# Edge stage of a graph kernel: the second product before the gathering of equal destinations, high casts on ScalarE, and the sort's numbering inside the stage

## What is computed

```python
e   = relu(edge_attr @ We1 + be1) @ We2 + be2            # 40000 x 256, hidden 512
msg = relu(layernorm(x)[src] + e)
out_h = segment_sum(msg, dst, num_segments=2500)
x = x + relu(((1 + eps) * layernorm(x) + out_h) @ Wn1 + bn1) @ Wn2 + bn2
```

## Time and profile before

| | us |
|---|---|
| median of 3 runs | 2723.11 (2719.55 to 2726.37) |
| the profiled execution | 2718.02 |
| its span | 2716.3 |

### The profile page before, as it was taken

One profiled execution on the slowest core, in us unless ns is written; L12 is line 12 of the kernel. 1 busy time (PEld: TensorE's weight loads), 2 busy tenths in 40 slices (PEclk: granted clock), 3 DMA queues, 4 the chain that ended last, 5 costly groups with the idle time before them and its releaser, 6 DMA issues. The chain is left out here.

```text
span 2716.3 us, 46328 instructions
## 1 busy us (share of the span) xinstructions
PE 2088.1 (77%) x13095; PEld 1804.4 (66%) x13096; DVE 1647.1 (61%) x4774; ACT 1007.2 (37%) x1931; POOL 1394.8 (51%) x1131
## 2 busy tenths in 40 slices
PE   2599999999999999955629999990466666662778
PEld 2588888888888888855628888880444444441776
DVE  5477786666666666648464444445655555557774
ACT  1254445545445554432205555550222222221321
POOL 1387887877777877760001111105377777771000
PEclk9799999999999999977759999995777767765888
DMA  6466656666666666642116777762233333342001
GB/s 165 134 131 131 133 120 130 134 132 135 135 128 125 133 130 133 129 86 70 39 41 229 244 243 242 239 220 81 76 92 93 90 89 91 90 84 28 22 10 38
DMA packets 185998, 325.71 MB, mean 120 GB/s; under 512 B 27528, under 2 KB 109037, under 8 KB 185192
## 3 DMA queue, kind: packets, MB, share of 16 engines
q0 software_dynamic: 82080, 141.73, 25.8%
q1 hardware_dynamic: 102962, 181.83, 21.8%
q10 hardware_dynamic: 900, 1.50, 0.2%
HBM read 260.65 MB, written 64.30 MB: 120 GB/s over the span
## 5 line engine op out<-in xcount | busy, mean ns | idle before, releaser
L632 POOL DMA_INDIRECT edge_sums<-edge_agg,edge_slot x316 | 551.3, 1745 | 172.5 <-issue 78.8
L1750 POOL DMA_INDIRECT att_got<-head_table,att_idx x352 | 401.8, 1141 | 125.1 <-issue 107.0
L623 POOL DMA_INDIRECT edge_nf<-node_table,edge_node_idx x316 | 327.3, 1036 | 152.0 <-issue 89.0
L751 ACT ACTIVATE edge_whole<-edge_h_ps,edge_b 128x512 f32<-128x512 f32 x316 | 215.8, 683 | 482.2 <-PE edge_h_ps L468 478.4
L466 PE MATMUL edge_e_ps<-edge_w_high,edge_hid_low 128*128 128x256 f32 x1264 | 357.3, 283 | 0.1
L467 PE MATMUL edge_e_ps<-edge_w_low,edge_hid_high 128*128 128x256 f32 x1264 | 356.9, 282 | 0.0
L468 PE MATMUL edge_e_ps<-edge_w_high,edge_hid_high 128*128 128x256 f32 x1264 | 356.2, 282 | 0.0
L1780 PE MATMUL att_s_ps<-att_w,att_hot 128*125 128x258 f32 x704 | 277.0, 562 | 3.2 <-issue 1.8
L466 PE MATMUL edge_h_ps<-edge_eat_high,edge_w_low 128*128 128x512 f32 x632 | 248.9, 394 | 23.6 <-DVE edge_eat_low L811 23.6
L1361 POOL DMA_INDIRECT moe_rows<-node_table,moe_idx x54 | 51.9, 961 | 396.8 <-DVE moe_idx L1473 396.4
L825 DVE TENSOR_TENSOR edge_pre<-edge_e_ps,edge_nf 128x1024 f32<-128x1024 f32 x79 | 96.8, 1225 | 256.2 <-DMA edge_nf<-node_table,edge_node_idx 208.9
(11 more groups left out here) (344 smaller groups left out, 4424.4 us busy)
## 6 DMA issues: line engine op xcount, KB each, us to landing
moe_w<-in_L_ffn_w_dram SPq DMA_DIRECT2D x162, 512.0 KB, 4.7
edge_ea<-in_edge_attr_dram SPq DMA_DIRECT2D x77, 448.0 KB, 5.1
edge_dst_row<-dst_rows SPq DMA_DIRECT2D x79, 256.0 KB, 4.5
routed<-moe_out SPq DMA_DIRECT2D x54, 128.0 KB, 6.3
att_got<-head_table,att_idx POOLq DMA_INDIRECT x352, 2.8
edge_nf<-node_table,edge_node_idx POOLq DMA_INDIRECT x316
edge_sums<-edge_agg,edge_slot POOLq DMA_INDIRECT x316, 4.8
edge_ea<-in_edge_attr_dram SPq DMA_DIRECT2D x77, 64.0 KB, 5.3
```

What stands on the lines that cost most here:

```text
L623: pool.indirect_dma_start(nf[u][:, j, :], None, m.node_table[:, :], bass.IndirectOffsetOnAxis(ap=node_idx[u][:, j:j + 1], axis=0)).then_in ...
L632: pool.indirect_dma_start(m.sums[k][:, :], bass.IndirectOffsetOnAxis(ap=slot[u][:, j:j + 1], axis=0), agg[u][:, j, :], None, compute_op=AL ...
L751: act.activation(whole[c][:], h_ps[:, c % 2, 0:N], ACT.Relu, bias=b1[:, c:c + 1]).then_inc(hid_whole, 1)
L1750: pool.indirect_dma_start(got[v][:, j, :], None, m.head_table[:, :], bass.IndirectOffsetOnAxis(ap=idx[v][:, j:j + 1], axis=0)).then_inc(la ...
```

## The change

- `edges_out(g)` stands ahead of `gather_same(g-1)` on TensorE, in all groups.
- ScalarE makes the high part of all four hidden pieces, each right after its relu, and the high part of the message after the fourth. VectorE's casts go.
- VectorE does `hidden_low` of pieces 0 and 1 ahead of `add_nodes(g-1)`, and `message_low(g-1)` after piece 3.
- The sort's numbering leaves `node_mlp`. After group 23 TensorE forms the totals in `h_ps` and waits until VectorE has read them (`offsets`); in groups 24 to 43 VectorE numbers one bucket each (`number_bucket`), and after that writes the slots out (`write_out`). TensorE's loop is cut in two there; VectorE's groups 22 to 43 are written out.
- The weights of `node_mlp` are loaded from ScalarE's queue.

```diff
@@ BucketSort
+    def offsets(self, dve, sums):
+        dve.wait_ge(self.summed, 1)
         chain.link(nc.vector.tensor_scalar(self.nblk_i[:], sums[0:LANES, 1, 0:buckets], (unit - 1) / 2, 1 / unit, ALU.add, ALU.mult))
+        chain.link(nc.vector.tensor_copy(off[:], sums[0:LANES, 0, 0:buckets]))
+        if self.by_bucket:
+            nc.vector.sem_inc(self.offsets_ready, 1)
...
+    def number_bucket(self, dve, b):
+        one = slot[:] if b == 0 else self.part_i[:].bitcast(F32)
+        units = self.m.count[0:1, 0:self.units]
+        last = self.last[0:1, b:b + 1]
+        chain.link(nc.vector.scalar_tensor_tensor(one, self.seen[:, b, :], self.off[:, b:b + 1], self.mask[:, b, :], ALU.add, ALU.mult))
+        if b == 0:
+            chain.link(nc.vector.tensor_scalar(tile_f[:], units, last, None, ALU.is_ge))
         else:
+            nc.vector.tensor_tensor(slot[:], slot[:], one, ALU.add)
+            chain.link(nc.vector.scalar_tensor_tensor(tile_f[:], units, last, tile_f[:], ALU.is_ge, ALU.add))
@@ edge_messages, TensorE
+    numbered = 2 + TILES + 2
...
+                edges_out(1)
                 pe.wait_ge(rows_made, 1)
                 gather_same(0, 0, first=True)
-                edges_out(1)
...
+                            edges_out(g + u)
+                            gather_same(g + (u - 1), 1 - u)
+                turns(2, numbered)
+                pe.wait_ge(hid_whole, numbered * KH)
+                by_src.order.totals(pe, h_ps)
+                pe.wait_ge(by_src.order.offsets_ready, 1)
+                turns(numbered, tail)
                 for g in range(tail, groups):
                     hidden(g)
                     if g + 1 < groups:
                         transposes((g + 1) % 2, ((g + 1) // 2 + 1) * 32)
+                    edges_out(g)
                     gather_same(g - 1, (g - 1) % 2)
-                    edges_out(g)
@@ ScalarE
                 for c in range(KH):
                     hidden_relu(g, c)
-                    if c == 1 and first != 1:
-                        message_high(g - 1)
-                    if c % 2 == 0:
-                        even_high(g, c)
+                    hidden_high(g, c)
+                if first != 1:
+                    message_high(g - 1)
@@ VectorE
             def hidden_low(g, c):
-                if c % 2 == 0:
-                    nc.vector.wait_ge(even_high_ready, g * (KH // 2) + (c // 2 + 1))
-                else:
-                    nc.vector.wait_ge(hid_whole, g * KH + (c + 1))
-                    nc.vector.tensor_copy(hidh[:, c, :], whole[c][:]).then_inc(odd_high_ready, 1)
-                    nc.vector.wait_ge(odd_high_ready, g * (KH // 2) + (c // 2 + 1))
+                nc.vector.wait_ge(hid_high_ready, g * KH + (c + 1))
...
+                    hidden_low(g, 0)
+                    hidden_low(g, 1)
                     add_nodes(1 - u, g - 1)
                     if ahead > 0:
                         stage_node_idx(1 - u, g + 1)
-                    hidden_low(g, 0)
-                    hidden_low(g, 1)
-                    message_low(g - 1)
                     hidden_low(g, 2)
                     hidden_low(g, 3)
+                    message_low(g - 1)
...
-                with dve.Fori(1 + TILES // 2, tail // 2) as turn:
+                for g in range(2 + TILES, numbered):
+                    one_group(g, g % 2)
+                by_src.order.offsets(dve, h_ps)
+                for g in range(numbered, numbered + TILES):
+                    one_group(g, g % 2)
+                    by_src.order.number_bucket(dve, g - numbered)
+                by_src.order.write_out(dve)
+                with dve.Fori((numbered + TILES) // 2, tail // 2) as turn:
@@ node_mlp
-                sp.dma_start(w1[:], io["Wn1"].rearrange("(k p) h -> p k h", p=P)).then_inc(w_in, 16)
...
-                by_src.order.number(dve)
...
+                act.dma_start(w1[:], io["Wn1"].rearrange("(k p) h -> p k h", p=P)).then_inc(w_in, 16)
...
-                by_src.order.totals(pe)
```

More of the change, by code:

```diff
@@ L275, in number @@
[L275 to L278 removed]
+        nc.tensor.matmul(sums[0:LANES, 0, 0:buckets], m.before[0:LANES, 0:LANES], self.mine[:], start=True, stop=True)
@@ L325, in _ @@
             def _(pe):
-                order.totals(pe)
+                order.totals(pe, order.sums)
             @block.vector
```

87 lines of the change are left out of this document (37 added, 50 removed).

## The result

The changed kernel takes **2745.8 us** (median of 4 runs, 2744.5 to 2753.1) against 2722.4 us (4 runs) before: 1.009 times the time, 95% interval 1.0068 to 1.0113. The forecast was 2685 us, with a range of 2645 to 2722. The sign was wrong.

The account below looks back on a forecast made before the run. The prediction took GpSimd, never resting in the edge stage at 14.07 us a group, as the bound. Steady part -30, start +5, numbering +3 and node stage -16 sum to -38 us from 2723.1: 2685 us, range 2645 to 2722.

Parts of the forecast that it names:

- steady part: 76 edge-stage groups at 13.7 us each in place of 14.1: -30 us (bounds -57 and +8).
- "These lie in its idle time": Numbering in 20 edge groups, 1.3 us each, hidden while VectorE waits for gathers; 26 us if the cover is gone.
- GpSimd's instructions without casts: Edge stage: without VectorE's casts GpSimd's adds and gathers take 0.6 us less a group, giving a floor of 13.1 us.
- x + B = 13.7: Edge group's pace: 6.8 us from `add_nodes` to the load, plus 6.9 from the load to the next `add_nodes`.
- its check: Two-group loop: 11.8 us first add to last gather, 5.4 gather, 10.2 `add_nodes` to first add; 27.4, again 13.7 a group.
- rival (c): Edge stage slower from late sums: two-group loop 29.5 us, 14.75 a group, +41 us in all, 2764 us; chance 0.14.
- gather + w: Gather's time plus an add's wait for a landing; from 6.4 us on the two-group loop reaches 14.2 a group.
- Start +5: GpSimd's first groups begin about 5 us later, the first gathering standing behind group 1's second product: +5 us (0 to 6).
- PE's wait for the offsets +3: TensorE waits once for `offsets_ready` in the edge stage, `hidden(24)` queued behind it: +3 us (0 to 6).
- Node stage -16: Node stage: third `combine` and TensorE's third turn 19.5 us earlier, less 3 us for slower clock: -16 us (-10 to -32).
- moving the weights "costs nothing": Node stage: moving three loads from SyncE's queue to ScalarE's costs nothing, since ScalarE has nothing else to do there.
- Rival (a): TensorE sets the edge pace, 13.35 us a group, if loads are early enough: -65 us in all, 2658 us; chance 0.20.

Follow-up runs that it names:

- e2: The changed kernel with the three edge edits undone, leaving the numbering in the edge stage and the node weights on ScalarE's queue: 2721.9 us, 1.001.
- e1: The kernel before with all edge edits (product order, casts on ScalarE, VectorE's and ScalarE's new orders), numbering left in the node stage: 2739.2 us, 1.0081.
- e13: The changed kernel with four slot buffers in place of two: 2739.7 us, 1.0056.
- e16: e14 with the sum of a bias to x in 20 pieces, one in each counting group, in place of one instruction: 2667.4 us, 0.9795.
- e4: The kernel before with only the high casts of all four tiles on ScalarE: 2735.1 us, 1.0056.
- e17: e14 with the odd high casts back on VectorE, ScalarE casting the even tiles only: 2681.8 us, 0.9866.
- e11: The changed kernel with edge rows loaded one group earlier and the node weights on SyncE's queue ahead of the sums: 2705.8 us, 0.9936.
- e14: The changed kernel with four slot buffers, edge rows loaded one group earlier and the node weights on SyncE's queue: 2672.1 us, 0.9805.
- e12: Old edge order, early edge rows, sorting in the edge stage, weights on SyncE's queue; `message_low` made a plain difference: 2693.1 us, 0.9891 (without that 0.9889).
- e5: The changed kernel with the sorting work ahead of `find_slots`' wait: eight of twelve runs 2724 to 2753 us (1.0046), four 2803 to 2838.
- e7: The kernel before with edge rows loaded one group earlier, ahead of the `dst_row` load: 2705.5 us, 0.9946.
- e3: The kernel before with only TensorE's order changed, second product ahead of gathering: 2922.8 us, 1.0759.
- e8: The kernel before with TensorE's and VectorE's orders changed, odd casts left on VectorE, message's high part after the second tile: 2954.6 us, 1.0859.

## Why the prediction was wrong, step by step

In short: the largest miss is the steady part, and in it the stretch B, from the load to the next `add_nodes`: forecast 6.9 us, measured 7.5. Over 76 groups that is 46 us. Two smaller ones are the numbering (11 us for the forecast's 3, for VectorE's idle time was taken as its cover) and the node weights (6.4 us gained of 16, for their move was put at nothing).

**"These lie in its idle time"** (numbering): failed for the order in which it was to be judged. It was true of the old order (e2: 1.001). The forecast took VectorE's idle share from before, 61% busy, but the change itself moves that idle time from ahead of `add_nodes` into `find_slots`, and the sorting work and the low parts stand behind it. The price was not 20 times 1.3 us but stood in two places, offsets 6.7 and writing out 4.5. In a third, the bias, the edge edits cost 5.0 (e1 has it without the numbering); the forecast didn't treat it, since the change doesn't touch it. Four slot buffers took the first two away (e13), pieces the third (e16). That a pause of TensorE in the edge stage is followed by matmuls at half the clock, 2.7 us at the offsets, was in no term; the forecast had the clock in the node stage alone.

**GpSimd's instructions without casts** (0.6 us a group, first add to last gather 11.8 us): failed. From first add to last gather it measured 12.6 us in the mean; of the 0.8 us more, 0.5 is in the adds, 0.1 in the gathers and 0.3 in the pauses between them. The row of 2.54 us with a cast in it showed that something beside an instruction lengthens it, not that the cast did: in the changed kernel an add of 2.68 us (1006.43) has no cast near. The Trainium skill's rule ("SBUF — State Buffer", two separate sides), by which a VectorE copy in a mode that takes both port pairs keeps GpSimd from writing descriptors, would have given up to 1.0 us a group, as the prediction has it. e4 and e17 show a loss of 0.35 us for GpSimd's adds in one order (4 x 0.087) and a gain of 0.17 in the other (4 x 0.042).

**x + B = 13.7**, and its check: x was right (6.8 us forecast and measured), B was 7.5, not 6.9. The forecast held B at 6.9 as long as the load is ahead of the gather. The loads were ahead, by 1.9 and 1.0 us (1.5 forecast), but the gather still took 5.6 us in the mean (5.4 forecast) and came later, since the stretch in front of it was longer. From `add_nodes` to the first add 10.4 (10.2). So the two-group loop is 12.6 + 5.6 + 10.4 = 28.6 us by the means of these parts, 14.3 a group, which is what the thirty groups from 44 on took; the forecast had 27.4. In e11, with the gather down to 3.5 us, the same parts are 12.2 + 3.5 + 11.3 = 27.0, and its groups there take 13.5. That is rival (c)'s loop, which was to take over from gather + w = 6.4 on; gather + w is 5.6 here, and what brings the loop to its length is the longer stretch from first add to last gather: the mechanism right, its deciding term another. Steady part: +16 us and the three places (16 more, the forecast's +3 in them), not -30; with the start (4.1) and all behind the last add (-7.6) that is the 28.5 us.

**Start +5**: 4.1. Right. **PE's wait for the offsets +3**: 4.2 us, but GpSimd's interval grew by 6.7; the slower clock behind the wait has 2.7 of it.

**Node stage -16, moving the weights "costs nothing"**: the sums' part of the step was right, the weights' was wrong. On ScalarE's queue they run beside the sums' loads, and the bias landed 26.6 us after its issue. With them on SyncE's queue the stage ends 15.0 us sooner after the last add than before (96.5 against 111.5): the -16 of the forecast. In the changed kernel 6.4.

**Rival (a)**, TensorE at 13.35 us "if the loads are far enough ahead": e14 and e16, where they are, run at 13.4, with 0.4 us of the wait for the last low part that was forecast at 0.45. The gather behind the edge rows took 5.4 us and without them 3.4: neither the full delay behind them nor none. The Trainium skill ("DMA: Bandwidth & Descriptors", queues, rings and completion order) has each DMA engine take turns between queues; the 5.4 us, between 3.4 and the 6.9 of a full wait, agree with sharing, and the share was got rid of by issuing the loads earlier.

What stays open: what lengthens GpSimd's instructions (e12 excludes one kind of neighbour; two SBUF inputs fit `message_low` and `add_nodes`, not `hidden_low`, and are not shown), and why e5's times fall into two sets.

## What to carry to other kernels

Reordering moves an engine's idle time, so ask, after the reorder, which wait it lies in and what is queued behind that wait; work is hidden only ahead of it. A change in an order that spans three engines is one unit: in parts it cost 203, 232 and 98 us here, whole 20, and with the sorting moved too 53 us less than before once the transfer that stood in the new loop and a two-deep buffer were out of the way. A pause of TensorE costs more than its length where the granted clock drops behind it. A load moved to another queue isn't free if it was first and now shares the DMA engines with large ones.

## What the runs showed of the hardware that was not expected

- A gather of node rows took 3.5 us in the mean (e7) with no edge rows (448 and 64 KB) issued beside it, and 5.4 with them (before); an add into a sum table took up to 8.8 us to land beside them (e13).
- Behind a pause of 4.2 us TensorE's granted clock was 0.50 from 434 to 440 us, and a hidden product took 8.3 us in place of 5.6. In the two slowest orders, in which TensorE waits most, the mean from 300 to 1100 us was 0.91 (e3) and 0.90 (e8).
- Three loads on a second queue, issued together with eight sum loads on SyncE's, landed 26.6 us after issue; ahead of the same loads on one queue 4.6 us.
- GpSimd's gather and add grow from 0.98 and 1.63 us to 1.86 (e12) and 2.68 (the changed kernel) beside a 128x1024 VectorE instruction with both inputs in SBUF, not beside one as long with one input in PSUM; when the casts are taken from VectorE the adds don't shrink in one order (e4) and shrink by 0.04 us in the other (e17 to e14). Beside the addition of 125x5120 elements one gather took 4.79 us.
